# Value products in tiles of 32 channels, and TensorE's code placed by two jumps a step

## What is computed

```
x = x + L0_xattn(layernorm(x), ctx)      # cross attention, 16 heads of 8
x = x + L0_ffn(layernorm(x), ...)        # first network, 6 layers
x = x + L1_xattn(layernorm(x), ctx)      # two-way cross attention with a gate
x = x + L1_ffn(layernorm(x), ...)        # second network, 2 layers
```

```
q, k, v = heads(shift(x) @ Wqkv)
q = rotate(l2norm(q) * q_scale); k = rotate(l2norm(k) * k_scale)
sim  = einsum('bhwie,bhwje->bhwij', q, look(k)) * 8     # look: this window and the last
attn = softmax(where(mask, -inf, sim))
out  = einsum('bhwij,bhwje->bhwie', attn, look(v))       # the value products
x = out @ Wo + x
```

## Time and profile before

| | us |
|---|---|
| median of 3 runs | 2175.77 |
| lowest, highest | 2172.82, 2176.37 |
| the profiled execution's own time | 2173.06 |
| its span, first to last instruction | 2171.3 |

### The profile page before, as it was taken

One profiled execution on the slowest core, in us unless ns is written; L12 is line 12 of the kernel. 1 busy time (PEld: TensorE's weight loads), 2 busy tenths in 40 slices (PEclk: granted clock), 3 DMA queues, 4 the chain that ended last, 5 costly groups with the idle time before them and its releaser, 6 DMA issues. The chain is left out here.

```text
span 2171.3 us, 88004 instructions
## 1 busy us (share of the span) xinstructions
PE 2076.2 (96%) x33646; PEld 1433.3 (66%) x33646; DVE 1829.7 (84%) x4895; ACT 1673.9 (77%) x5828; POOL 1389.0 (64%) x1318
## 2 busy tenths in 40 slices
PE   7998999999999999999999999999999787899997
PEld 5665766667666666667666676666666565666665
DVE  4889988889898889889888889888896587888873
ACT  4667888888888888888888888888887335787784
POOL 1337777767777777777676777767774226666660
PEclk9999999999999999999999999999999988999999
DMA  4001222122211222112221222112121100000000
GB/s 118 4 3 31 75 63 50 44 53 69 62 47 44 68 61 53 44 46 76 62 50 44 53 66 62 44 45 63 50 52 38 30 18 6 14 16 11 16 9 27
DMA packets 144806, 97.05 MB, mean 45 GB/s; under 512 B 61976, under 2 KB 137408, under 8 KB 144384
## 3 DMA queue, kind: packets, MB, share of 16 engines
q1 hardware_dynamic: 143232, 91.02, 16.6%
q10 hardware_dynamic: 1152, 0.26, 0.1%
HBM read 23.11 MB, written 1.05 MB: 11 GB/s over the span
## 5 line engine op out<-in xcount | busy, mean ns | idle before, releaser
L739 PE MATMUL bank<-wqkv,hs 128*128 128x512 f32 x1344 | 657.7, 609 | 5.0 <-ACT arena L1593 2.5
L1982 POOL TENSOR_TENSOR arena<-arena,rnorm 128x512 f32<-128x512 f32 x448 | 455.3, 1045 | 278.3 <-DVE rnorm L259 277.0
L1975 POOL TENSOR_TENSOR arena<-arena 128x512 f32<-128x512 f32 x448 | 565.9, 1274 | 57.6 <-DVE arena L2195 57.6
L1622 ACT ACTIVATE arena<-bank,amx 128x64 f32<-128x64 f32 x1536 | 457.5, 331 | 27.1 <-DVE amx L2252 26.8
L739 PEld LDWEIGHTS bank<-wqkv,hs 128*128 128x128 f32 x1344 | 229.6, 191 | 177.7 <-issue 157.7
L1622 ACT ACTIVATION_READ_ACCUMULATOR arena<-bank,amx 128x1 f32 x1536 | 346.0, 225 | 0.0
L2195 DVE TENSOR_TENSOR arena<-bank,rot 128x256 f32<-128x256 f32 x896 | 334.8, 416 | 0.0
L2190 DVE TENSOR_TENSOR arena<-bank,rot 128x512 f32<-128x512 f32 x448 | 307.2, 686 | 22.6 <-PE bank L739 20.3
L1599 ACT ACTIVATE arena<-bank 128x512 f32<-128x512 f32 x426 | 249.6, 621 | 87.9 <-PE bank L760 87.8
L760 PEld LDWEIGHTS bank<-ident,arena 128*128 128x128 f32 x1792 | 212.0, 141 | 156.7 <-issue 112.4
L1989 POOL TENSOR_TENSOR arena<-arena,ainv 128x512 f32<-128x512 f32 x192 | 200.3, 1043 | 166.7 <-DVE ainv L2260 166.7
(11 more groups left out here) (227 smaller groups left out, 3309.1 us busy)
## 6 DMA issues: line engine op xcount, KB each, us to landing
arena<-arena SPq DMA_DIRECT2D x768, 64.0 KB, 2.5
wqkv<-in_L_ffn_Wqkv_dram SPq DMA_DIRECT2D x24, 256.0 KB, 3.3
hs<-z SPq DMA_DIRECT2D x128, 32.0 KB, 2.0
hs<-z SPq DMA_DIRECT2D x128, 31.8 KB, 1.9
fx<-z SPq DMA_DIRECT2D x31, 128.0 KB, 2.2
fx<-z SPq DMA_DIRECT2D x31, 127.0 KB, 2.5
wqkv<-in_L_ffn_Wqkv_dram SPq DMA_DIRECT2D x24, 128.0 KB, 2.7
w<-in_L_ffn_W_dram SPq DMA_DIRECT2D x6, 341.0 KB
```

What stands on the lines that cost most here:

```text
L739: nc.tensor.matmul(bank[o][:], src[:], wqkv[w][:, off:off + 512], start=True, stop=True).then_inc(AT[name] if part < 2 else AT[name][i], 1)
L1622: ins = nc.scalar.activation(pb[i][0][p % 2][:, h * DH:(h + 1) * DH], bank[3 + g][:, j * DH:(j + 1) * DH], ACT.Exp, bias=amx[p % 2][:, i, ...
L1975: nc.gpsimd.tensor_tensor(t, t, rs[i][c], ALU.add).then_inc(AT["ak" if c else "aq"][i], 1)
L1982: nc.gpsimd.tensor_tensor(t, t, rnorm[p % 2][:, i, HU * c:HU * c + HU].unsqueeze(2).to_broadcast([P, HU, DH]), ALU.mult).then_inc(AT["mk" ...
```

## The change

`values_all` splits the 64 channels of each product into two parts of 32, so the 24 products become 48, each from 64 rows to 32 partitions; what is multiplied and where the sums land is the same. The single jump of odd steps is replaced by two in every step: one behind the queries of unit 0 (place 98), one where the old one stood (place 81).

```diff
-FETCH_BLOCK, SCORES_AT = 256, 60
+FETCH_BLOCK, FIRST_AT, SECOND_AT = 256, 98, 81
...
                     for j in range(2):
                         for (q0, q1), src in sources:
-                            for half in range(2):
+                            for half, part in itertools.product(range(2), range(2)):
                                 for g in range(2):
-                                    rows, to, h = slice(DH * g, DH * g + DH), DH * (g ^ half), j + 2 * half
-                                    mm = nc.tensor.matmul(bank4[7 - half][to:to + DH, j, q0:q1], src[g][rows, DH * h:DH * h + DH],
+                                    rows, h = slice(DH * g, DH * g + DH), j + 2 * half
+                                    to, d = DH * (g ^ half) + 32 * part, DH * h + 32 * part
+                                    mm = nc.tensor.matmul(bank4[7 - half][to:to + 32, j, q0:q1], src[g][rows, d:d + 32],
                                                           pbt[i][0][rows, h * P + q0:h * P + q1], start=True, stop=True)
...
                         queries(0, s)
+                    if live(s - 3) and live(s):
+                        pe.addr_align(FETCH_BLOCK, offset=FIRST_AT, max_nops=0)
...
                     feed_forward_0(s, 1)
-                    if live(s - 3) and live(s - 1) and s % 2:
-                        pe.addr_align(FETCH_BLOCK, offset=SCORES_AT, max_nops=0)
+                    if live(s - 3) and live(s - 1):
+                        pe.addr_align(FETCH_BLOCK, offset=SECOND_AT, max_nops=0)
```

More of the change, by code:

```diff
@@ L1 @@
+import itertools
 from contextlib import ExitStack
```

## The result

The changed kernel takes 2297.72 us (median of 4 runs, 2296.81 to 2300.37) where the kernel before, run beside it, takes 2174.3: the ratio is 1.058, with an interval of 1.0562 to 1.0597. It is slower, as forecast, but by 123 us and not by 27, and the time lies outside the range of 2150 to 2245.

A forecast was written before the change was run, and what follows sets the result against it. TensorE (PE) was taken as the bound, in the first network's stage. 2173.06 + 21 (values) + 0 (borders) + 7 (jumps) = 2201, taken as 2202 us, 1.2% slower; range 2150 to 2245, likeliest case 2180 to 2225 (0.45).

The forecast's parts named there:

- What bounds the kernel: First network's 96 steps: PE idles 9 us of 1440.0, so its gains or losses move the end by as much.
- Part 1: Values in 32-channel tiles: 96 loads at 8.8 ns, +0.14 us a burst, less 0.03, x 192: +21 us (-17 to +71).
- What the equal tile shape was to give back: Between last score load and first value load: 0.03 of the 0.09 us gap comes back, ends 0 and 0.09.
- Part 2: Where code blocks end within the bursts: 0 taken, ends about 15 us saved or 13 us lost.
- rival C: Much slower: values at 12.0 ns a load, or next block late at score borders (93 x 0.4); 2225 to 2260, chance 0.20.
- Part 3: Jumps, 47 become 187: those behind the queries cost 0 to 14 us, +7 taken; those at the old place 0.
- The cover of 1.86 us: Projection work queued behind the queries hides that much of the jump; against 2.02 us about 0.15 us shows.
- The SECOND jump: Behind the output projection, where the old jump stood: some 1.78 us queued covers it, cost 0.

The follow-up runs named there:

- Run 10: The kernel before without its one jump in odd steps: 2242.49 us, ratio 1.0324.
- run 4: The changed kernel computing only the first 32 channels of each value product, 48 loads of 32 columns a burst: 2259.35 us (one run).
- run 5: The changed kernel with half of each value product's moving columns (queries) left out: 2303.87 us (one run).

## Why the prediction was wrong, step by step

**What bounds the kernel: right.** Three terms on PE add up to 121.5 of the 123 us, so PE's losses reached the end of the kernel.

**Part 1, the pace of a 32-column load: mis-sized.** It was read as 8.8 ns from a stretch of 0.07 us inside the scores, and gave +0.14 us a burst. In the steady part of an undisturbed value group pairs mostly start 8.3 ns apart, so the pace was right to a tenth. It was a favourable reading, though: the stretch beside it

```profile
845.25:845.35 0.10, 0.10 (x19) 1.00 0.68 164
```

gives (0.10 + 0.105)/19 = 10.8 ns by the same rule. What failed is the step that multiplies 8.8 by 96 and adds nothing. Starts of passes in one undisturbed group of the changed kernel (from 745.249 us), counted from the first, in ns:

```
pass     1    9   17   25   32   33   34   35   36   40   60   80   96
start    0   56  131  178  215  241  296  304  339  388  566  722  917
```

Up to pass 32 the passes start 6.9 ns apart; from 32 to 36 it takes 124 ns, and from there to 96 it is 9.6 ns on average (8.3 ns and some longer steps). Counted from the records, the pairs whose load has begun and whose pass hasn't ended (ends of passes are modelled) rise to 33 and never above, in the whole trace of each of the thirteen kernels. In this group they reach 33 with the 33rd load, 189 ns in, and the next load starts 56 ns later. My reading is that a dense group runs ahead until about 64 instructions are out and then stands. It doesn't give the pace behind the standstill: from pass 36 to pass 60 only some 11 to 26 pairs are out, and the pace is 8.3 ns and more all the same. The cap wasn't tested by itself. The least sizes follow without it: an undisturbed value group takes 1.038 us from first pass to next work where it took 0.831, +0.207 us a burst, 40 us in all. The other 0.11 us a burst are disturbances: the mean group lies 0.132 us over the least one, where before it lay 0.022 over it. Most of that is a second standstill of 0.11 us in the mean, seen behind pass 60 in three quarters of the groups (145 of 192; in the burst shown above, PE starts nothing from 816 to 922 ns after the group's first pass). It is more frequent where a code packet starts between 0.3 and 1.17 us into the group (112 of 137) than elsewhere (33 of 55), which points at the fetch without proving it.

The Trainium skill (TensorE: Matmul & The Clock Gate, Architectural detail, on engine queue depths) gives 64 as the depth of TensorE's queue. The 33 pairs counted here are at most 63 loads and passes in the kernel before and 65 in the changed one, close to that; I hadn't drawn on it.

What the equal tile shape was to give back, 0.03 us: between the loads, where it was forecast, the gap of an undisturbed burst went from 0.09 to 0.04 us, but from last score pass to first value pass it takes 0.127 us where it took 0.145. So 0.018 us came, 3.5 us in all, and the 17 us that the Trainium skill's rule on tiling modes (TensorEngine Tiling (Array Packing), Key Properties) could have brought did not.

**Part 2, borders: mis-sized.** +8.5 us for 0, inside the ends of 15 us either way. Clean score groups fell from 0.771 to 0.753 us (the gap just named), but 31 of 95 first bursts take 1.1 to 1.7 us, with the border at the last passes, and stand there. Their FIRST jumps are as long as the others' (2.4 and 2.3 us). What differs is the work behind them: all 31 are among the 46 bursts that begin 2.1 to 2.6 us after the jump's end, and none among the 49 that begin 2.9 us or more after it. They leave the jump's block before the next is there. That is the mechanism of rival C's second half, and C's 2.4 us was read rightly; its price of 93 x 0.4 = 37 us was about twice what these bursts lost (0.98 us in the mean of all 95 against 0.81 in the undelayed ones, 17 us, in part made up by cleaner scores elsewhere).

**Part 3, the jumps: the wrong kind of number.** The cover of 1.86 us was right: 1.98 us of projections run over the jump shown above. The jump was priced as an operation of 2.0 us, from the only crossing one in the trace. It isn't one. It took 2.32 us in the mean (1.40 to 3.06), since it ends with the arrival of the next block, 3.2 to 4.35 us after its own block was entered. The prediction had what was needed, that the jump "arrives soon after its block was entered", and used it to choose between 0.29 and 2.02, not to work out an end. The single one of before was such a wait itself: it ends 1.36 us after its packet, like the FIRST jumps here. The step that failed is taking one instance of a wait for its length. +7 should have been +53.

The rule cited there from the Trainium skill (Runtime: NRT & Kernel Launch, Instruction fetch mechanics), that a branch out of the pages at hand forces a fetch, fits the kind of wait seen here, but as it was used it leads to the same 2.0 us and the same error. Run 10 shows that plain running on into the next block costs as much when it comes too early.

**The SECOND jump: right.** It took 1.06 us in the mean where it crossed, and the time around it isn't beyond the usual 0.43 us in the mean.

**The rivals.** C held both mechanisms, values slower than paced and blocks not there in time, but as alternatives and with 93 x 0.4. They came together: 60 + 53 + 8.5. As priced, neither reaches C's upper end (2173 + 192 x 0.34 = 2238, 2202 + 93 x 0.4 = 2239), and even that end, 2260, was 38 us short. In the range, half of C's top was cut off.

**What would have been needed.** The prices of both parts were within reach in the trace of before. The score group itself, 64 pairs of 32 columns in 0.77 us, is longer than 64 x 8.8 = 0.56; taken whole it gives rival C's 12.0 ns, 1.16 us for 96 pairs, and 1.17 was measured. So close a match is partly luck: an undisturbed group takes 1.04, and the rest is disturbance that the score group doesn't have. I set the 12.0 aside as "its slow start and its tail", and part of it repeats in every group.

**What stays open.** Why a packet starts anywhere between some 0.6 and 2.4 us after the jump's block was entered, which decides between a jump of 1.4 and one of 3.1 us. What the standstill behind pass 60 is. Why 48 narrow pairs on 4 tiles (run 4) start slower than the first 48 of 96 on 8 tiles. Whether places exist at which the split kernel has no waits at all; even then it would carry the +0.207 us a burst, 40 us.

## What to carry to other kernels

Splitting small products doubles their code as well as their count (282 blocks became 377 by the split alone), and a stage of dense small products can be bound by how fast its code arrives: work out the time between two borders of code blocks, and where it is under some 4 us, as measured in this kernel, expect PE to stand there, jump or no jump. Take the price of a wait from what ends it, never from its length in one place; and price a group of many small instructions by a whole group, start and tail included. A jump over padding pays where it keeps two borders apart (70 us in the kernel before, 140 in the changed one) and costs where it brings them together (97 us for the two jumps without the split), and its place is worth a scan: 74 entries were worth 63 us.

## What the runs showed of the hardware

- A jump out of a block that was entered shortly before ended 3.0 to 4.7 us after the first pass of that block, with medians of 3.6 to 3.9 us in five kernels. Running on over the border has to wait as well (1.2 to 1.9 us shown here), and goes on 1.2 to 1.65 us after a code packet has landed. A crossing FIRST jump ends 1.37 us (1.25 to 1.55) after one; the packets ahead of these jumps take 0.9 to 1.6 us.
- Moving a jump later doesn't get rid of the wait: it stood at the next border (42 us less at the jump, 42 us more in the scores).
- Float32 pairs of load and pass from 64 rows: 14.5 ns on average with 64 columns; with 32 columns on 8 tiles 32 pairs at some 7 ns, 0.12 us for the next four, and then 8.3 to 9.6 ns. Half the moving columns leave the steady 8.3 ns as they are and take 0.1 us off 96 pairs (run 5).
- Never more than 33 pairs were under way, from the start of the load to the (modelled) end of the pass, in all thirteen traces.
